# An instruction order of its own for each engine, keys and values in separate tiles, a third key buffer, and all key placing issued from SyncE, in the fourth attention layer of an eight-image kernel

## What is computed

```python
h = group_norm(x); x = h + softmax(q(h) k(h)^T * C**-0.5) v(h)             # layer 0: 256 tokens, one head
x = gamma1 * softmax(relu q . relu k within each row of 16) v(x) + x       # layer 1: windows of 16
x = gamma2 * softmax(q k^T) v(x) + x                                       # layer 2: 256 tokens, 16-wide q, k
xp = avg_pool_3x3_s2_same(x)                                               # layer 3: 64 pooled tokens
qt = (x @ w_q + b_q).reshape(BS * 8, 256, 16)                              # 8 heads, by a plain reshape
kt, vt = (xp @ w_k + b_k).reshape(BS * 8, 64, 16), (xp @ w_v + b_v).reshape(BS * 8, 64, 16)
out = softmax(qt kt^T / 4) vt
x = out.reshape(8, 16, 16, 128) @ w_o + b_o + x
```

## Time and profile before

| | us |
|---|---|
| runs without the profiler | 133.01, 131.18, 129.76 (median 131.18) |
| the profiled execution, its own time | 131.21 |
| its span, first to last instruction | 129.4 |
| outside the span | 1.81 |
| TensorE busy, share of the span | 111.2, 86% |
| VectorE, ScalarE, GpSimd busy | 81.6, 76.6, 66.8 |

### The profile page before, as it was taken

How to read it: one execution, slowest core, us unless ns; L and a number is a source line. 1 busy time by engine, 2 the same in 40 slices (tenths; PEclk the granted TensorE clock), 3 DMA queues, 4 the chain that set the end, 5 groups by cost and what they waited for, 6 DMA issues and landing times.

```text
span 129.4 us, 3874 instructions
## 1 busy us (share of the span) xinstructions
PE 111.2 (86%) x1516; PEld 86.3 (67%) x1516; DVE 81.6 (63%) x201; ACT 76.6 (59%) x228; POOL 66.8 (52%) x116
## 2 busy tenths in 40 slices
PE   6687999999999999999989999848943996949881
PEld 4465899987876878767668797526413675739780
DVE  4867767554324464588878823459699299888112
ACT  0445397698884756648796837165617637474450
POOL 8303629898801211321018988872977929963000
PEclk9999999999999999999999999998698599995999
DMA  3960000000000000000000027244565560120123
GB/s 74 331 211 0 0 5 3 0 3 3 0 5 0 5 0 0 5 0 0 0 0 0 5 72 133 77 100 123 107 91 122 105 62 5 46 79 2 51 75 88
DMA packets 15521, 6.43 MB, mean 50 GB/s; under 512 B 9360, under 2 KB 14864, under 8 KB 15504
## 3 DMA queue, kind: packets, MB, share of 16 engines
q1 hardware_dynamic: 13744, 4.66, 16.4%
q10 hardware_dynamic: 1760, 1.53, 4.5%
HBM read 4.61 MB, written 1.57 MB: 48 GB/s over the span
## 4 chain that ended last, share of the span: by engine, by line
PE 60%; DVE 16%; ACT 13%; DMA 4%; POOL 3%; issue 2%; ACTq 0%; DVEq 0%
PE bank L794 10%; PE bank L739 9%; DVE negmax L618 6%; PE bank L758 5%; ACT prob L488 5%; PE bank L832 5%; PE bank L846 4%; ACT probT L492 4%; DMA x_all<-in_x_dram 4%; PE bank L778 4%; PE bank L791 3%; DVE prob L621 3%; PE bank L730 3%; PE bank L819 3%; PE bank L723 2%; PE bank L768 2%
## 5 line engine op out<-in xcount | busy, mean ns | idle before, releaser
L432 ACT ACTIVATE prob<-bank,negmax 128x256 f32<-128x256 f32 (+1 forms) x48 | 19.3, 409 | 13.3 <-DVE negmax L583 10.4
L610 DVE SCALAR_TENSOR_TENSOR xT<-bank,packed,xT 128x256 f32<-128x256 f32 x24 | 11.6, 483 | 16.1 <-PE bank L794 12.1
L488 ACT ACTIVATE prob<-prob 128x512 f32<-128x512 f32 x16 | 9.8, 631 | 15.3 <-DVE prob L621 15.3
L794 PE MATMUL bank<-probT,v 128*128 128x256 f32 x64 | 16.9, 387 | 0.4 <-ACT probT L470 0.4
L739 PE MATMUL bank<-packed,xT 128*128 128x128 f32 (+1 forms) x96 | 15.6, 286 | 0.2 <-ACT prob L432 0.2
L375 POOL TENSOR_TENSOR prob<-prob,inv 128x512 f32<-128x512 f32 x14 | 14.4, 1051 | 0.5 <-DVE inv L631 0.5
L739 PEld LDWEIGHTS bank<-packed,xT 128*128 128x128 f32 x96 | 13.1, 191 | 1.9 <-issue 1.2
L360 POOL TENSOR_TENSOR probT<-turned,packed 128x256 f32<-128x256 f32 x8 | 4.9, 612 | 18.4 <-DVE turned L605 18.4
L368 POOL TENSOR_TENSOR probT<-prob 128x512 f32<-128x512 f32 x8 | 10.2, 1269 | 7.6 <-ACT prob L488 7.6
L846 PE MATMUL bank<-probT,vdiag 128*32 128x32 f32 x512 | 6.8, 206 | 7.9 <-ACT probT L492 7.8
L794 PEld LDWEIGHTS bank<-probT,v 128*128 128x128 f32 x64 | 11.2, 190 | 3.2 <-issue 1.6
(11 more groups left out here) (111 smaller groups left out, 237.4 us busy)
## 6 DMA issues: line engine op xcount, KB each, us to landing
kdiag<-k_rows SPq DMA_DIRECT2D x28, 64.0 KB, 2.2
out_dram<-x_all SPq DMA_DIRECT2D x8, 128.0 KB, 1.9
x_all<-in_x_dram SPq DMA_DIRECT2D x2, 256.0 KB, 4.2
x_all<-in_x_dram ACTq DMA_DIRECT2D x2, 256.0 KB, 5.5
vdiag<-v_rows SPq DMA_DIRECT2D x8, 64.0 KB, 3.3
packed<-in_pack_dram ACTq DMA_DIRECT2D x1, 321.0 KB, 5.8
k_rows<-kT SPq DMA_DIRECT2D x4, 64.0 KB, 1.9
kdiag<-k_rows ACTq DMA_DIRECT2D x4, 64.0 KB, 3.4
```

The costliest lines, as they stand in the source:

```text
L432: last = nc.scalar.activation(prob[g][:, t, 0:keys], psum("scores", layer, g)[:, keys * t:keys * t + keys], ACT.Exp, bias=negmax[g][:, t, ...
L488: nc.scalar.activation(prob[g][:, t, :], prob[g][:, t, :], ACT.Exp).then_inc(s_exp3, 1)
L794: last = mm(ps[:, 0:TOK], vals[:, k, 0:C], probT[g][:, 0, TOK * k:TOK * k + TOK], start=k == 0, stop=k == TILES - 1)
```

## The change

`sequence` is gone. A table `slots` gives each engine its own order. Up to layer 2's first projections the orders are those of before, but for "setup" (two small VectorE steps earlier). Beyond that:

- TensorE, end of layer 2: the pairs of scores stand behind one or two more projections and updates than before (scores of images 4 and 5 now follow v of image 7 and probT of image 1, where they preceded both), and bias stands behind them, ahead of the first product of layer 2. On VectorE the four bias operations stand between the scaling of image 3 and the maximum of image 5.
- Layer 3: probT3 of an image stands two scores steps behind its own on ScalarE (exponentials of image 2, then read-outs of probT3 of image 0), where it stood three behind. ScalarE's read-out of pv of image 0 now stands ahead of the exponentials of image 4. At the end both turnings, of images 6 and 7, stand ahead of pv of image 6.
- Keys and values have separate steps, tiles and projections; the value projection of the last pair stands behind y of image 3 on TensorE.
- `KEY_BUFFERS` is 3: a third kdiag, zeroed by GpSimd after the second at the start, and the wait of the third pair is gone; the fourth pair waits for the scores of image 1.
- SyncE issues all 32 key transfers. Its order is now write keys 0, place keys 0, write keys 1, write values 0, place keys 1, write keys 2, place keys 2, write values 1, place values 0, place values 1, write keys 3, place keys 3, write values 2, store 0, place values 2, write values 3, stores 1 to 3, place values 3, stores 4 to 7.
- GpSimd zeroes the four vdiag tiles behind layer 1's last window instead of behind layer 0's last scaling.

```diff
-KEY_BUFFERS = 2
+KEY_BUFFERS = 3
...
+        slots = {
+            "tensor": {
...
+                ("scores", 2): [73, 79, 85, 91],
+                ("probT", 2): [82, 84, 88, 90, 95, 99, 102, 105],
+                ("bias", 3): [86],
+                ("o", 2): [87, 89, 94, 96, 100, 103, 110, 112],
+                ("x", 3): [92, 97, 106, 107, 121, 134, 139, 140],
+                ("q", 3): [93, 101, 108, 111, 113, 114, 118, 126],
+                ("k", 3): [98, 104, 116, 120],
+                ("v", 3): [109, 122, 125, 146],
+                ("scores3", 3): [115, 117, 119, 123, 127, 131, 137, 141],
+                ("probT3", 3): [124, 129, 130, 136, 142, 148, 151, 152],
+                ("pv", 3): [128, 133, 135, 138, 147, 150, 153, 155],
+                ("y", 3): [132, 143, 144, 145, 149, 154, 156, 157],
+            },
+            "scalar": {
...
+                ("scores3", 3): [93, 95, 97, 101, 104, 109, 111, 116],
+                ("probT3", 3): [99, 103, 105, 110, 115, 118, 119, 121],
+                ("pv", 3): [102, 106, 108, 114, 117, 120, 122, 123],
+            },
+            "vector": {
...
+                ("v", 3): [80, 87, 90, 101],
+                ("scores3", 3): [83, 84, 86, 89, 92, 94, 97, 99],
+                ("share3", 3): [85, 88, 91, 93, 95, 98, 104, 105],
+                ("y", 3): [96, 100, 102, 103, 106, 108, 109, 110],
+                ("last3", 3): [107],
+            },
+            "gpsimd": {
...
+                ("late", 3): [24],
+                ("pool", 3): [25, 26, 27, 28, 29, 30, 31, 32],
+                ("halves3", 3): [33, 34, 36, 39, 41, 42, 45, 46],
+                ("share3", 3): [35, 37, 38, 40, 43, 44, 47],
+            },
+            "sync": {
+                ("write keys", 3): [0, 2, 5, 10],
+                ("place keys", 3): [1, 4, 6, 11],
+                ("write values", 3): [3, 7, 12, 15],
+                ("place values", 3): [8, 9, 14, 19],
+                ("store", 3): [13, 16, 17, 18, 20, 21, 22, 23],
+            },
+        }
...
             def place_keys(i):
...
-                    sp.wait_ge(s_zero, QUARTERS + IMAGES // PAIR)
+                    sp.wait_ge(s_zero, ZEROS)
...
-                for c in range(SHARED if i == 0 else HEADS):
+                for c in range(HEADS):
                     place_chunk(sp, i, c)
...
-            for n in range(EARLY, QUARTERS - LATE):
+            for n in range(EARLY, KEY_BUFFERS):
                 clear_kdiag(nc.gpsimd, n)
...
-                    if g == 1:
-                        act.wait_ge(s_zero, QUARTERS + IMAGES // PAIR)
-                        act.wait_ge(s_keys_out[0], 16)
-                        for c in range(SHARED, HEADS):
-                            place_chunk(act, 0, c)
...
+            def keys3(g):
+                rows = pooled(g)
+                mm(begin("k", 3, g)[:, 0:PAIR * PTOK], part["w3k"], rows, start=True, stop=True).then_inc(*filled_by("k", 3, g))
+            def values3(g):
+                rows = pooled(g)
+                mm(begin("v", 3, g)[:, 0:C], rows, part["w3v"], start=True, stop=True).then_inc(*filled_by("v", 3, g))
```

More of the change, by code:

```diff
@@ L149, in build @@
-        due, start = [], 0
-        for n, (kind, layer, distance) in enumerate(steps):
-            start += distance
-            for g in range(IMAGES):
-                if kind != "kv" and (kind, layer) not in (("qk", 1), ("qk", 2)):
-                    due.append((start + g, -n, kind, layer, g))
-                elif g % 2:
-                    due.append((start + g, -n, kind, layer, g - 1))
-        sequence = [task[2:] for task in sorted(due)]
-        sequence.insert(sequence.index(("qk", 1, 0)), ("setup", 1, 0))
@@ L166, in build, with turns_of @@
+        def turns_of(engine):
+            every = []
+            for (step, layer), row in slots[engine].items():
+                every += [(slot, step, layer, IMAGES // len(row) * n) for n, slot in enumerate(row)]
+            return [task[1:] for task in sorted(every)]
+        turns = {engine: turns_of(engine) for engine in slots}
         order = [("xT", 0, 0), ("xT", 0, 2)]
@@ L229, in width_of, with nth @@
             return C + 1 if layer == 0 else C
-        def nth(step, layer, g):
-            return [(s, l, n) for s, l, n in sequence if s == step].index((step, layer, g)) + 1
+        def nth(step, layers, layer, g):
+            return [(l, n) for s, l, n in turns["vector"] if s == step and l in layers].index((layer, g)) + 1
         def strip_of(g, n):
@@ L330, in _, with clear_values @@
                 nc.gpsimd.tensor_scalar(part[w], part[w], part[gate], None, ALU.mult).then_inc(s_gated, 1)
-            def clear_late():
-                for late in range(QUARTERS - LATE, QUARTERS):
-                    clear_kdiag(nc.gpsimd, late)
+            def clear_values():
                 for i in range(IMAGES // 2):
                     nc.gpsimd.memset(vdiag[i][:, :, :, :], 0.0).then_inc(s_zero, 1)
-            for step, layer, g in sequence:
-                if step == "scores" and layer == 0:
+            for step, layer, g in turns["gpsimd"]:
+                if step == "scores":
                     pool.wait_ge(s_raw, g + 1)
@@ L457, in _ @@
             nc.scalar.activation(part["w0r"], fuse[:, C + 2:C + 3], ACT.Copy, scale=float(C) ** -0.5).then_inc(s_fused, 1)
-            for step, layer, g in sequence:
+            for step, layer, g in turns["scalar"]:
                 if step == "norm":
                     normalise(g)
-                if step == "qk" and layer > 0:
+                if step == "qk":
                     queries_keys(layer, g)
@@ L657, in _ @@
             factors(HALF)
-            for step, layer, g in sequence:
-                if step == "qk" and layer == 0 and g >= EARLY_QUERIES:
+            for step, layer, g in turns["vector"]:
+                if step == "qk" and g >= EARLY_QUERIES:
                     queries_keys0(g)
```

160 lines of the change are left out of this document (93 added, 67 removed), and 4 rows, old and new, of the table slots.

## The result

After the change the median is 131.18 us (128.37 to 134.73, 20 runs), beside 131.49 us for the kernel before (129.76 to 134.19, 20 runs). The ratio of the two is **0.9883, with a 95% interval of 0.9839 to 0.9927**: 1.2% faster, where 4.4% was forecast. Medians here are over all runs and ratios over the undisturbed ones, and the rows of before, e2, e5, e6, e8, e11, e12, e13 and e17 come from disturbed executions, so medians, ratios and rows need not agree. The profiled execution took 129.24 us (span 127.4), 3.8 us above the forecast of 125.4.

The account below looks back on a forecast made before the run. No engine is full in layer 3; the common order's in-order waits bound the kernel. Last addition 120.5 plus 0.8 for the clock is 121.3 against 127.14, 5.8 us less: 131.21 to 125.4 us, range 121.8 to 129.3.

Parts of the forecast that it names:

- Start: Start and layers 0 and 1: GpSimd's second zeroing of 3.51 us fits its idle time, 1.9 us stay free; cost 0.
- End of layer 2: TensorE's and VectorE's new order there makes the update of image 0 1.0 us later, between 0 and 1.5.
- First keys: Layer 3, first pair: keys placed by SyncE alone set the scores of image 0 at 82.4, 0.9 us later.
- Second pair: Layer 3: key rows written at 80.2, eight chunks in 3.5 us, keys landing near 87.5 to 88.5, as before.
- VectorE's walk from image 5 on: Layer 3: scores of images 5 to 7 at 100.7, 105.0, 108.3; last multiplication ends at 116.2, 2.5 us earlier.
- Third buffer: Layer 3 key placing: a third key buffer is worth nothing by itself.
- Tail: End of layer 3: both turnings ahead of pv 6 remove a 2.9 us lap; last addition at 120.5 before the clock term.
- Clock: TensorE in layer 3: a second low clock spell falls on the scores of image 5, adding 0.8 us (0 to 2).
- The rival in which placing bounds the kernel: Layer 3: SyncE alone issues every pair's chunks at 0.57 us each, giving 128.8 us; chance 0.16.
- a placing of well over 4 us: SyncE's key placing: eight chunks needing well over 4 us would show the prediction wrong.
- the end of layer 2 later by more than 1.5 us: The end of layer 2 sliding by more than 1.5 us would show the prediction wrong.
- pv 6 waiting for the last values: Tail: values were forecast to land near 117.0, about when pv 6 wants them; a wait would show the prediction wrong.

Follow-up runs that it names:

- e2: The changed kernel with TensorE's steps up to layer 2 and the bias step in the order of the kernel before; ratio to the kernel before 0.9781.
- e5: The changed kernel with the second pair's key projection behind the queries of image 3 on TensorE and ScalarE; ratio to the kernel before 0.9919.
- e6: The changed kernel with the edits of e2 and e4 together; ratio to the kernel before 0.9717.
- e8: The changed kernel with two key buffers instead of three; ratio to the kernel before 0.9881.
- e11: The changed kernel with the edits of e1, e2 and e4 together; ratio to the kernel before 0.9709.
- e12: e4 with the last pair's values projected right behind the third pair's, and written and placed ahead of all stores; ratio to the kernel before 0.9836.
- e13: e10 with TensorE's steps up to layer 2, and bias, in the order of the changed kernel; ratio to the kernel before 0.9733.
- e17: e6 with GpSimd's halves ahead of multiplications, scores of images 5 and 6 earlier on TensorE, exponentials of image 5 earlier on ScalarE; ratio to the kernel before 0.9716.
- e9: The kernel before with ScalarE's order alone changed: exponentials of an image behind the read-out of turned probabilities three images earlier; ratio to the kernel before 0.9752.
- e3: The kernel before with only the turning of image 7 moved ahead of pv of image 6, read-out included; ratio to the kernel before 0.9875.
- e10: The kernel before with the edits of e9 and e3 together; 126.64 us, ratio to the kernel before 0.9604.
- e1: The changed kernel with ScalarE again issuing half of the first pair's key chunks; ratio to the kernel before 0.9881.
- e4: The changed kernel with the first values placed ahead of the third pair's keys on SyncE; ratio to the kernel before 0.9694.
- e7: The changed kernel with matmuls on zeros, 24 ahead of the wait for the second pair's keys, 16 ahead of the first values; ratio to the kernel before 1.0138.
- e18: e17 with ScalarE sharing the first pair's key placing as in e1; ratio to the kernel before 0.9725.

## Why the prediction was wrong

The forecast had the right two gains and the wrong price for the rest. Alone on the kernel before they give 2.5% (e9) and 1.25% (e3), together 4.0% (e10), against 4.4% forecast for the whole change. The other parts take back 2.8%, the difference between after and e10. Against my times the profiled run is late by 1.6 us at the scores of image 0 (85.11 beside 83.5), by 2.3 at image 2, 2.8 at image 5, 4.2 at image 6, 4.2 at the end of the last multiplication and 3.9 at the last addition.

- *Start: right.* GpSimd zeroed two diagonals in 6.96 us, and 1.86 us of idle time stayed ahead of the first power operation, at 9.71 (9.81 in the earlier trace rows).
- *End of layer 2: mechanism right, term mis-sized.* I took 1.0 us; the update of image 0 slid by 0.65 and that of image 1 by 1.55, just past my upper bound. I had followed image 0, while the first pair's keys need image 1. VectorE's list has the maximum of image 6 ahead of that update, and the scores it needs now stand behind the product of image 1 on TensorE: VectorE waited 1.34 us for them (70.16). Undoing it in after gave 1.0% (e2); for e10 the size is not shown (e13).
- *First keys: wrong resource.* I let the keys set the scores of image 0 at 82.4. They ran at 83.93, and earlier keys did not move them (e1), while less work ahead of them did (e5). TensorE, which came late out of layer 2, was busy right up to them. Keys did not set them before either: there the matmuls of the scores waited twice, 2.3 us for the keys of the second pair and 0.6 us, ahead of image 0 at 81.48, for ScalarE's read-out of the queries (busy and mean ns, then idle time):

```profile
L819 PE MATMUL bank<-kdiag,qT 64*32 64x256 f32 x256 | 10.1, 430 | 3.0 <-DMA kdiag<-k_rows 2.3 <-ACT qT L443 0.6
```

- *Second pair: mis-sized by 2 us.* Scores of image 2 at 90.22 instead of 88: the key write went out at 81.54 and not 80.2, and the eight issues took 4.87 us, the value of the slow placing in the earlier trace rows, where I took 3.5. Bringing these scores forward by 2.1 us won at most 0.8 us at the end (e1).
- *The failed step: VectorE's walk from image 5 on.* It let pv 0 stand ahead of the scores of image 5 with "values placed near 97" as if this were free. The second of the two transfers was issued at 95.18 and landed at 99.64, after 4.46 us (the median of the earlier trace rows is 3.3), and pv 0, which TensorE had reached at 97.45, waited 2.23 us until 99.68. My walk of SyncE's queue gave the write of the second pair's values, which stands ahead of this placing, no wait; it waits for VectorE's read-out, and e1 shows that this alone holds the placing until 93.95. Behind pv 0 in TensorE's list stood two turnings and then the scores of image 5. The removed wait for ScalarE was replaced by one for a transfer. Undoing that alone gives 1.9% (e4), the largest single loss: with image 2 as late as in after (91.30) the last multiplication ends at 118.91, 1.4 us earlier. The loss of image 6 belongs to the same walk: pv 2 and a stop of 1.12 us stand ahead of its scores.
- *Third buffer: right*, nothing (e8). *Tail: right.* From the end of the last multiplication to the last addition I had 4.3 us, measured 4.8; the last values delay pv 6 by 0.36.
- *Clock: wrong sign, small.* I added 0.8 us for a second low spell on the scores of image 5. It did not come: the one low spell of after lies at 90 to 96 us (0.50 in 92 to 94), behind the 3.12 us standstill, and from 96 us on, the 2.23 us wait of pv 0 included, the grant was 1.00. e7 shows that the clock was not the limit.

The rival in which placing bounds the kernel gave 128.8 us, close to the measured 129.24, but not by its mechanism: of the four placings of eight chunks one was slow (4.87 us; the others took 3.54 to 3.57). Three of the prediction's own signs of being wrong did show: a placing of well over 4 us, the end of layer 2 later by more than 1.5 us, and pv 6 waiting for the last values.

Why undoing the losses does not add up: each hides behind the other. With layer 2 and the values mended (0.972), GpSimd's hand-over shows (1.05 us twice in e6); with that mended, TensorE's order (1.19 us); with that mended, the fourth pair's keys (2.73 us in e18, 4.30 in e17). These waits are shown. That mending the last one too would reach e10's 0.960 is only argued, and stays open.

## What to carry to other kernels

When an order is rewritten for one wait, list for the step that was waiting every other input and when it arrives: the gain ends at the second latest. Make the two moves that the profile asks for first and alone; here seven lines gave 4.0%, and the full table of orders 1.2%. A transfer in an in-order queue is an instruction like any other: place it by when its reader needs it, and put another transfer into the time in which a write travels.

## What the runs showed of the hardware

A single DMA issue on SyncE, 0.4 us as a rule (0.65 for a placing of values), takes 1.5 to 1.7 us in a few places, and an instruction transfer falls in the same time. In after, the window 85.5 to 87.6, where one of the eight issues took 1.73 us (from 85.74), has this queue line (packets, MB, share):

```profile
q8 instruction: 1, 0.02, 4.1%
```

Before has the same at 83 to 85 in its 4.60 us placing of the earlier trace rows (one issue of 1.48 us), so the "slow" placing is no property of the chunks. That the instruction transfer causes the long issue is an inference from the times falling together, and no run tested it.

TensorE, too, stops with no semaphore to wait for ("issue" in the rows: 1.12 us in after, up to 1.84 in e12), and the stops move when instructions are added or moved ahead of them. Here the times do not fall together: no instruction transfer lies in 105.5 to 106.8 us of after, nor in any of the four stops of e12. What causes these stops, and how much of the time of e7 and e12 they cost, stays open.

The clock granted to TensorE early in the program differs between the profiled executions, with the same order up to there: 1.00 in 12 to 16 us in one group, 0.68 to 0.73 in the other, and layer 2's first update comes 1.6 to 2.1 us later with it. That is as much as the whole change gained.
